# Attention scores with queries on the partitions, and the weights turned by transposing transfers

## The chip, the core and the metric

The kernel runs on one NeuronCore of a Trainium2 chip. A core has TensorE (PE, the matrix engine; PEld is its weight loading), VectorE (DVE), ScalarE (ACT), GpSimd (POOL), SyncE (SP, which here only issues transfers) and 16 DMA engines. Each engine works through its own instruction stream in order; streams meet only at semaphores. The metric is the time of one execution on the device in microseconds. The kernel before takes 780.97 us (median of 3 runs, 780.57 to 782.66).

## The reference

One transformer layer on x of shape (2, 1024, 256): layernorm, causal attention with 16 query heads and 4 key/value heads over low-rank latents, an int8-quantised feed-forward block, and both added to x. The change lies in the attention:

```
q = concat([q_nope, rope(q_rope)])   # 16 heads, 128 + 64 wide
k = concat([k_nope, rope(k_rope)])   # 4 heads, each used by 4 query heads
attn = einsum('bhqd,bhkd->bhqk', q, k) * scale
attn = where(causal, -inf, attn)     # keys after the query are masked
attn = softmax(attn, axis=-1)
out  = einsum('bhqk,bhkd->bhqd', attn, v) @ W_o
```

The kernel works in the latent space: keys are 64 rotated and 64 latent rows, values are 64 latent columns and a column of ones, which gives the sum of the softmax beside the product.

## The kernel before

**Stages.** A prologue makes the latents, joined weights and first queries; a loop of 32 steps (4 key heads x 2 batches x 4 query heads) does the attention; the feed-forward block stands at the end. Small pieces of other work (rounding and turning of integers, rotated keys of later heads, the output product) are spread over the loop through one PSUM bank, `misc`, used in turns by TensorE and one reader (`misc_of`, `misc_used`, `misc_full`).

**A step** handles 1024 queries against 1024 keys, of which the causal half is computed: 8 tiles of 128 keys, 36 blocks of 128 x 128. Precision is bought by splitting: queries, keys and weights are each a high and a low part.

- TensorE first computes, a step or two ahead, the scores with high parts only and queries on the partitions (`max_unit`), into two banks `pmax`. VectorE takes each row's masked maximum (`maxima`, line 863). A transposition of 8 columns (line 1234), a split into two bf16 rows (lines 870, 872) and two transfers (line 368) turn the maxima into a row `m_row` along the queries.
- `scores` then computes the scores with **keys on the partitions**: per strip of up to 512 queries a mask product for the diagonal, a pass that adds minus the maximum (`ones_b` x `m_row`) and three passes, high x high, low x high and high x low. There are 12 strips in a step, in three banks that rotate.
- ScalarE takes the exponential twice (lines 684, 685): rounded to f16 as the high part `p_hi`, and in full in PSUM. VectorE subtracts the two to get `p_lo` (line 996).
- With keys on the partitions the weights already lie as the value product wants them: `values` multiplies each block of `p_hi`, `p_hi`, `p_lo` by 65, 64 and 65 columns of values, into the `head` banks. VectorE divides by the sum (`normalise`).
- GpSimd rotates the queries (lines 469 to 478, 4 instructions) and makes their low part (line 484), two to three steps ahead of their use; `q_hi` has three buffers.

Every fourth step has the output product of two pairs of heads (4 tiles, lines 1278 to 1290); the even steps but the first turn the normalised output (line 1275).

## Time and profile before

| what | value |
|---|---|
| median of the 3 runs | 780.97 us (780.57 to 782.66) |
| the profiled execution's own time | 779.53 us |
| its span | 777.7 us |
| PE busy | 729.5 us, 94% |
| DVE busy | 580.6 us, 75% |
| ACT busy | 496.3 us, 64% |
| POOL busy | 420.4 us, 54% |
| bytes moved by DMA | 33.08 MB |

The span runs from the first to the last instruction; the execution's own time holds 1.8 us around it. Busy is the union of an engine's instructions. A PE instruction is shown from its start to the end of its results, so neighbours overlap; what it costs the engine is the distance to the start of the next. The same holds, by less, on ACT and DVE.

### The profile page before, as it was taken

How to read it: one execution, taken by the hardware profiler on the slowest of the kernel's cores; microseconds unless marked ns; L12 is line 12 of the kernel's file. 1: busy time of each engine (PE TensorE's matmuls, PEld its weight loads, DVE VectorE, ACT ScalarE, POOL GpSimd, SP SyncE). 2: the span in 40 equal slices, each digit the busy share in tenths (PEclk: the TensorE clock that was granted, in tenths of full speed). 3: DMA queues.
4: the chain of work that ended last, by engine and by line, in shares of the span. 5: the costliest groups of instructions: out<-in, count | busy, mean ns of one | idle time of the engine just before them, and what ended most of it. 6: DMA issues, size and time to landing. Idle time of an engine off the chain costs nothing.

```text
span 777.7 us, 18089 instructions
## 1 busy us (share of the span) xinstructions
PE 729.5 (94%) x7010; PEld 582.9 (75%) x7084; DVE 580.6 (75%) x1530; ACT 496.3 (64%) x1015; POOL 420.4 (54%) x210
## 2 busy tenths in 40 slices
PE   7996699899999999999999999999999999999856
PEld 5664468688876678878877888788878888887635
DVE  6748478887777777777777768776777787776796
ACT  3555467577556565767577657765776577657754
POOL 4323546666655554676467646764676467620225
PEclk9786699999999999999999999999999999999989
DMA  9754002001300200010001000100000000000003
GB/s 261 256 201 178 1 1 82 16 15 42 124 1 29 82 28 2 21 43 23 2 1 30 1 15 16 42 15 2 1 29 2 1 2 2 2 1 3 14 0 109
DMA packets 20517, 33.08 MB, mean 43 GB/s; under 512 B 2704, under 2 KB 11472, under 8 KB 20304
## 3 DMA queue, kind: packets, MB, share of 16 engines
q1 hardware_dynamic: 19648, 31.34, 12.8%
q8 instruction: 56, 0.92, 0.5%
q10 hardware_dynamic: 784, 0.59, 0.3%
q14 instruction: 29, 0.24, 0.1%
HBM read 21.30 MB, written 10.49 MB: 41 GB/s over the span
## 4 chain that ended last, share of the span: by engine, by line
PE 78%; DVE 10%; issue 4%; ACT 4%; DMA 2%; POOL 1%; SPq 0%; POOLq 0%; ACTq 0%; DVEq 0%
PE psum L1078 74%; PE psum L1275 2%; DMA acc<-in_L_attn_x 2%; DVE hid L1058 1%; DVE small L1027 1%; ACT psum L685 1%; DVE p_lo L996 1%; POOL res L521 1%; ACT p_hi L684 1%; DVE acc L755 1%; PE psum L1101 1%; ACT hid L711 0%; PE psum L1326 0%; DVE kt_a L960 0%; PE psum L1234 0%
## 5 line engine op out<-in xcount | busy, mean ns | idle before, releaser
L684 ACT ACTIVATE p_hi<-psum 128x512 f16<-128x512 f32 (+3 forms) x384 | 187.7, 489 | 169.8 <-PE psum L1078 164.6
L996 DVE TENSOR_TENSOR p_lo<-psum,p_hi 128x512 f16<-128x512 f32 (+3 forms) x384 | 208.4, 553 | 85.7 <-ACT psum L685 84.5
L863 DVE CUSTOM_DVE_ANT_0 junk<-psum,cmask 128x1024 bf16<-128x1024 f32 (+7 forms) x256 | 187.8, 752 | 58.9 <-issue 57.4
L469 POOL TENSOR_TENSOR q_swap<-q_raw,sin_sb 32x1024 f32<-32x1024 f32 x31 | 73.6, 2374 | 228.9 <-ACT q_raw L613 220.5
L685 ACT ACTIVATE psum<-psum 128x512 f32<-128x512 f32 (+3 forms) x384 | 187.2, 487 | 0.0
L1078 PE MATMUL psum<-q_hi,k_hi 128*128 128x512 f32 (+2 forms) x384 | 187.0, 487 | 0.0
L1078 PEld LDWEIGHTS psum<-kv_tok,p_hi 128*128 128x128 f16 x2304 | 116.9, 97 | 53.4 <-issue 38.6
L1078 PE MATMUL psum<-kv_tok,p_hi 128*128 128x65 f16 (+1 forms) x2304 | 151.9, 196 | 0.4 <-DVE p_lo L996 0.4
L1078 PE MATMUL psum<-kv_tok,p_lo 128*128 128x65 f16 x1152 | 138.1, 192 | 0.0
L1078 PE MATMUL psum<-q_hi,k_lo 128*128 128x512 f32 (+2 forms) x384 | 132.1, 344 | 0.0
L1078 PE MATMUL psum<-q_lo,k_hi 128*128 128x512 f32 (+2 forms) x384 | 131.9, 343 | 0.0
L1078 PE MATMUL psum<-k_hi,q_hi 128*128 128x512 f32 (+3 forms) x384 | 106.0, 358 | 11.7 <-DVE small L863 7.7
L1078 PEld LDWEIGHTS psum<-kv_tok,p_lo 128*128 128x128 f16 x1152 | 109.0, 100 | 0.0
L1078 PE MATMUL psum<-m_row,ones_b 128*128 128x384 bf16 (+2 forms) x313 | 100.8, 322 | 1.4 <-DVE p_lo L996 1.4
L1078 PEld LDWEIGHTS psum<-k_hi,q_hi 128*128 128x128 f32 x384 | 65.5, 192 | 32.2 <-DVE small L863 21.3
L484 POOL TENSOR_TENSOR q_lo<-q_raw,q_hi 128x1024 fp32r<-128x1024 f32 x32 | 76.8, 2401 | 15.9 <-PE psum L1078 10.8
L1078 PEld LDWEIGHTS psum<-q_lo,k_hi 128*128 128x128 f32 x384 | 72.7, 189 | 7.3
L1078 PEld LDWEIGHTS psum<-q_hi,k_lo 128*128 128x128 f32 x384 | 73.8, 192 | 4.3
L472 POOL TENSOR_TENSOR q_swap<-q_raw,sin_sb 32x1024 f32<-32x1024 f32 x31 | 74.0, 2388 | 2.4
L475 POOL TENSOR_TENSOR q_raw<-q_raw,cos_sb 64x1024 f32<-64x1024 f32 x31 | 73.9, 2382 | 2.4
L478 POOL TENSOR_TENSOR q_raw<-q_raw,q_swap 64x1024 f32<-64x1024 f32 x31 | 73.6, 2375 | 2.4
L1078 PEld LDWEIGHTS psum<-q_hi,k_hi 128*128 128x128 f32 x384 | 73.9, 193 | 0.0
(172 smaller groups left out, 1205.8 us busy)
## 6 DMA issues: line engine op xcount, KB each, us to landing
wq_split<-w_split SPq DMA_DIRECT2D x4, 1024.0 KB, 5.5
k_rotated<-k_split SPq DMA_DIRECT2D x8, 512.0 KB, 3.7
wq<-wq_split SPq DMA_DIRECT2D x16, 256.0 KB, 2.7
acc<-in_L_attn_x SPq DMA_DIRECT2D x4, 512.0 KB, 7.7
ffn_t<-in_L_attn_W_o SPq DMA_DIRECT2D x1, 2048.0 KB, 20.7
k_hi<-k_rotated SPq DMA_DIRECT2D x8, 256.0 KB, 4.0
k_lo<-k_rotated SPq DMA_DIRECT2D x8, 256.0 KB, 4.5
w_split<-in_L_ffn_w SPq DMA_DIRECT2D x2, 1024.0 KB, 6.0
```

Of the source, the lines that this page charges most:

```text
L469: pool.tensor_tensor(q_swap[0:HR, :], raw[HR:ROPE, :], sin_sb[HR:ROPE, :], ALU.mult)\
L472: pool.tensor_tensor(q_swap[HR:ROPE, :], raw[0:HR, :], sin_sb[0:HR, :], ALU.mult)\
L475: pool.tensor_tensor(raw[0:ROPE, :], raw[0:ROPE, :], cos_sb[0:ROPE, :], ALU.mult)\
L478: pool.tensor_tensor(raw[0:ROPE, :], raw[0:ROPE, :], q_swap[:, :], ALU.add).then_inc(S["pool_step"], 1)
L484: pool.tensor_tensor(q_lo[s % 2][:, :], q_raw[s % 2][:, :], q_hi[n % QRING][:, :], ALU.subtract)\
L521: pool.tensor_tensor(y[:, :, :], y[:, :, :], acc[:, t:t + 2, :], ALU.add).then_inc(S["f_res"], 1)
L684: act.activation(p_hi[j % PRING][:, o:o + used], src, ACT.Exp, scale=SCALE)
L685: act.activation(src, src, ACT.Exp, scale=SCALE).then_inc(S["exp_done"], 1)
L863: ins = dve.tensor_tensor_reduce(junk[:, o:o + w], pmax[:, o:o + w], cmask[:, T - w:T], 1.0, LOWEST, ALU.add, ALU.max, mcol[:, s % 2, i:i ...
L996: dve.tensor_tensor(p_lo[j % PRING][:, o:o + used], score[c % SBANKS][:, w - used:w], p_hi[j % PRING][:, o:o + used], ALU.subtract).then_i ...
L1078: ins = pe.matmul(dst, lhs, rhs, start=start, stop=stop, skip_group_check=True)
L1275: ins = pe.transpose(misc[:, i * P:(i + 1) * P], o_norm[:, 4 * k + i, :], identf[:, :])
```

## The change

The separate pass for maxima goes, with `pmax`, `m_row`, `m_cast`, their transposition and transfers. The three-pass scores are computed with **queries on the partitions**. VectorE reduces each tile's scores to the negative maximum (line 875 of the new kernel), which ScalarE takes as the bias of the exponential. Now the weights lie the wrong way for the value product and have to be turned:

- the four wide query tiles (7, 6, 5, 4: 1024, 896, 768, 640 keys) keep two exponentials and a subtraction; high and low part stand side by side in one of three buffers `p_src`, and **one transposing DMA per tile** (SP, line 369) turns both into `pt_big`: 512, 448, 384 and 320 KB, 26 blocks of each part per step;
- the four narrow tiles (3 to 0, 10 blocks) take one exponential in f32 into `p_f32`; VectorE makes both halves at once (`small_halves`: a cast, line 891, and a subtraction, line 893, of 1280 columns); TensorE transposes the 20 blocks through `misc` in turns of 8, 8 and 4, and ScalarE copies them to `pt_small` (line 688).

Wide tiles use two regions of PSUM alternately, the narrow ones one bank. The value products of tiles 6, 5, 4 and of the narrow tiles come in the next step; those of tile 7 at the end of the same step. The lookahead of the queries shrinks: queries are projected two steps ahead instead of three, `q_hi` has two buffers, and GpSimd rotates one step ahead. The output product's four tiles are spread over two steps, and a step's leftovers follow the last one. The scale moves from the exponential to the copy of the queries.

```diff
@@ tables
+UNITS = ((7,), (3,), (6,), (2,), (5,), (1, 0), (4,))
+NS = len(UNITS)
+BIG = {7: 0, 6: 1, 5: 2, 4: 3}
+SMALL = {3: 0, 2: 1, 0: 2}
+NB = len(BIG)
+MAX_AT = {i: k for k, i in enumerate(i for unit in UNITS for i in unit)}
+PSRC = 3
+COLS = {7: 0, 5: 0, 6: 2 * CH, 4: 2 * CH + P, 3: 4 * CH, 2: 4 * CH, 1: 4 * CH, 0: 4 * CH + 2 * P}
+KEYS = {7: (CH, CH), 6: (CH, CH - P), 5: (CH, 2 * P), 4: (CH - P, 2 * P), 3: (CH,), 2: (CH - P,), 1: (2 * P,), 0: (2 * P,)}
+OFF = {3: 0, 2: 4 * P, 1: 7 * P, 0: 9 * P}
+WB = 10 * P
+BLOCKS = [(h, i, j) for h in range(2) for i in (3, 2, 1, 0) for j in range(i + 1)]
+TURNS_B = [BLOCKS[k:k + 8] for k in range(0, len(BLOCKS), 8)]
+PV_AT = {0: (6, 1), 2: (5, 1), 3: (4, 1), 6: (7, 0)}
+PV_SMALL = 4
+PV_DONE = {7: 1, 6: 2, 5: 3, 4: 4}
+PV_STEP = 5
...
@@ SyncE
-            def row_of_maxima(n, s):
-                sp.wait_ge(S["m_cast_done"], n + 1)
-                for k in range(2):
-                    sp.dma_start(m_row[s % 2][k:k + 1, :], m_cast[:, k, :]).then_inc(S["m_row_in"], 16)
+            def turn_big(n, i):
+                q, w = NB * n + BIG[i], (i + 1) * P
+                if n:
+                    sp.wait_ge(S["pv_done"], PV_STEP * (n - 1) + PV_DONE[i])
+                sp.wait_ge(S["lo_done"], q + 1)
+                sp.dma_start(pt_big[i][:, :, :], p_src[q % PSRC][:, 0:2 * w], transpose=True)\
+                  .then_inc(p_in[q % PSRC], 16)
...
@@ GpSimd
-            rotate(2, 2, 6)
             for n in range(LAST):
+                if n + 1 < LAST:
+                    rotate(n + 1, n + 1, misc_index(n - 1, "query", 1) + 1 if n else 4)
                 for _, kind, k in misc_of(n):
                     if kind == "kb":
                         keys_low(k)
-                if n + 3 < LAST:
-                    rotate(n + 3, n + 3, misc_index(n, "query", 1) + 1)
-                if n + 2 < LAST:
-                    pool.wait_ge(S["score_done"], NC * (n + 1))
-                    query_low(n + 2, n + 2)
+                if n + 1 < LAST:
+                    query_low(n + 1, n + 1)
...
@@ ScalarE
-                            act.activation(p_hi[j % PRING][:, o:o + used], src, ACT.Exp, scale=SCALE)
-                            act.activation(src, src, ACT.Exp, scale=SCALE).then_inc(S["exp_done"], 1)
+            def exponentials(n, u):
+                for i in UNITS[u]:
+                    w, nb = (i + 1) * P, sm["mcol"][:, NT * (n % 2) + i:NT * (n % 2) + i + 1]
+                    src = psum[:, COLS[i]:COLS[i] + w]
+                    act.wait_ge(S["max_done"], NT * n + MAX_AT[UNITS[u][-1]] + 1)
+                    if i in BIG:
+                        q = NB * n + BIG[i]
+                        if q >= PSRC:
+                            act.wait_ge(p_in[q % PSRC], 16 * (q // PSRC))
+                        act.activation(p_src[q % PSRC][:, 0:w], src, ACT.Exp, bias=nb)
+                        act.activation(src, src, ACT.Exp, bias=nb).then_inc(S["exp_done"], 1)
+                    else:
+                        if n:
+                            act.wait_ge(S["small_lo"], n)
+                        ins = act.activation(p_f32[:, OFF[i]:OFF[i] + w], src, ACT.Exp, bias=nb)
+                        if i in SMALL:
+                            ins.then_inc(S["small_free"], 1)
+            def small_turned(k, idx):
+                act.wait_ge(S["misc_full"], idx + 1)
+                m = len(TURNS_B[k])
+                act.activation(pt_small[:, 8 * k:8 * k + m, :],
+                               misc.bitcast(F16)[:, 0:m * P].rearrange("p (t q) -> p t q", q=P), ACT.Copy)\
+                   .then_inc(S["misc_used"], 1)
...
@@ VectorE
-            def maxima(n, s, u):
-                dve.wait_ge(S["max_done"], USES * n + (u + 1))
-                dve.memset(sm["tick"], 0.0)
-                for i, o in MAX_UNITS[u]:
-                    w = (i + 1) * P
-                    ins = dve.tensor_tensor_reduce(junk[:, o:o + w], pmax[:, o:o + w], cmask[:, T - w:T], 1.0, LOWEST,
-                                                   ALU.add, ALU.max, mcol[:, s % 2, i:i + 1])
-                ins.then_inc(S["max_read"], 1)
+            def maxima(n, u):
+                dve.wait_ge(S["score_done"], NS * n + u + 1)
+                for i in UNITS[u]:
+                    dve.tensor_reduce(sm["mcol"][:, NT * (n % 2) + i:NT * (n % 2) + i + 1],
+                                      psum[:, COLS[i]:COLS[i] + (i + 1) * P], AX.X, ALU.max, negate=True)\
+                       .then_inc(S["max_done"], 1)
+            def big_low(n, i):
+                q, w = NB * n + BIG[i], (i + 1) * P
+                dve.wait_ge(S["exp_done"], q + 1)
+                dve.tensor_tensor(p_src[q % PSRC][:, w:2 * w], psum[:, COLS[i]:COLS[i] + w], p_src[q % PSRC][:, 0:w],
+                                  ALU.subtract).then_inc(S["lo_done"], 1)
+            def small_halves(n):
+                dve.wait_ge(S["small_free"], len(SMALL) * (n + 1))
+                if n:
+                    dve.wait_ge(S["misc_full"], misc_index(n, "pt", 2) + 1)
+                dve.tensor_copy(p_small[:, 0, :], p_f32[:, :]).then_inc(S["small_hi"], 1)
+                dve.wait_ge(S["small_hi"], n + 1)
+                dve.tensor_tensor(p_small[:, 1, :], p_f32[:, :], p_small[:, 0, :], ALU.subtract).then_inc(S["small_lo"], 1)
...
+            for n in range(LAST + 1):
+                s, r = n % STEPS, n % REP
+                for j in range(NS):
+                    if n < LAST:
+                        if j == 4:
+                            big_low(n, 6)
+                            if n:
+                                normalise(n - 1, 1)
                         if j == 6:
-                            turned = misc_index(n, "turn", 1) + 1 if r % 2 == 0 and n > 0 else None
-                            normalise(2 * n + 2, NT * n + PRING + 4, 0, s % 2, turned)
-            end = LAST
-            normalise(2 * end + 1, NT * end + PRING, 1, 1, None)
-            dve.wait_ge(S["pv_done"], NT * end + PRING)
+                            big_low(n, 5)
+                        maxima(n, j)
+                        if j == 2:
+                            big_low(n, 7)
+                    elif j == 4:
+                        normalise(n - 1, 1)
+                    if n and j == 0:
+                        big_low(n - 1, 4)
+                    if n and j == 5:
+                        normalise(n - 1, 0)
...
+                    if n < LAST and j == 6:
+                        small_halves(n)
...
@@ TensorE
-                mm(o, ones_b[:, 0:P], m_row[s % 2][:, qs], not diagonal, False)
-                mm(o, k_hi[b][:, ks], qh[:, qs], False, False)
-                mm(o, k_lo[b][:, ks], qh[:, qs], False, False)
-                mm(o, k_hi[b][:, ks], ql[:, qs], False, True, S["score_done"])
+                    qs, k0 = slice(i * P, (i + 1) * P), 0
+                    for w in KEYS[i]:
+                        ks = slice(k0, k0 + w)
+                        o = psum[:, COLS[i] + k0:COLS[i] + k0 + w]
+                        diagonal = k0 <= i * P < k0 + w
+                        if diagonal:
+                            mm(o[:, i * P - k0:(i + 1) * P - k0], ident[:, :], cmask[:, :], True, False)
+                        mm(o, qh[:, qs], k_hi[b][:, ks], not diagonal, False)
+                        mm(o, qh[:, qs], k_lo[b][:, ks], False, False)
+                        ins = mm(o, ql[:, qs], k_hi[b][:, ks], False, True)
+                        k0 += w
+                ins.then_inc(S["score_done"], 1)
...
+            def turn_small(m, k, idx):
+                pe.wait_ge(S["small_lo"], m + 1)
+                pe.wait_ge(S["misc_used"], idx)
+                for t, (h, i, j) in enumerate(TURNS_B[k]):
+                    o = OFF[i] + j * P
+                    ins = pe.transpose(misc.bitcast(F16)[:, t * P:(t + 1) * P], p_small[:, h, o:o + P], ident16[:, :])
+                ins.then_inc(S["misc_full"], 1)
```

How VectorE's stream reads around the start of a step before (`junk` and `m_cast` belong to the maxima, `ISA` is the masked maximum and its read-out):

```order
L996 TENSOR_TENSOR p_lo0<-psum,p_hi0 128x512 [waits pv_done,exp_done]
L870 TENSOR_SCALAR m_cast<-psum 8x128 [waits m_row_in,max_done]
L872 SCALAR_TENSOR_TENSOR m_cast<-psum,m_cast 8x128 [waits m_split]
L996 TENSOR_TENSOR p_lo1<-psum,p_hi1 128x384 [waits m_cast_done,pv_done,exp_done]
L860 MEMSET small 128x1 [waits max_done]
L863 ISA junk,small<-psum,cmask 128x1024
L863 ISA small 128x1
L996 TENSOR_TENSOR p_lo2<-psum,p_hi2 128x256 [waits pv_done,exp_done]
L888 RECIPROCAL small<-psum 128x4 [waits pv_done]
L892 TENSOR_TENSOR o_norm<-psum,small 128x4x64 [waits norm_step]
```

and in the changed kernel, from the halves of the narrow tiles of one step (`p_small`) into the next:

```order
L891 CAST p_small<-p_f32 128x1280 [waits misc_full,small_free]
L893 TENSOR_TENSOR p_small<-p_f32,p_small 128x1280 [waits small_hi]
L875 TENSOR_REDUCE small<-psum 128x1 [waits score_done]
L883 TENSOR_TENSOR p_src1<-psum,p_src1 128x640 [waits exp_done]
L875 TENSOR_REDUCE small<-psum 128x1 [waits score_done] x2
L883 TENSOR_TENSOR p_src2<-psum,p_src2 128x1024 [waits exp_done]
L916 TENSOR_TENSOR acc<-psum,acc 128x512 [waits acc_in,misc_full]
L875 TENSOR_REDUCE small<-psum 128x1 [waits score_done]
L883 TENSOR_TENSOR p_src0<-psum,p_src0 128x896 [waits exp_done]
L900 RECIPROCAL small<-psum 128x4 [waits pv_done]
L904 TENSOR_TENSOR o_norm<-psum,small 128x4x64 [waits norm_step]
L875 TENSOR_REDUCE small<-psum 128x1 [waits score_done]
```

The low parts stood one behind another with maxima of later steps between them; now each maximum and low part belongs to the step itself, and the halves of the narrow tiles stand between tile 4's maximum and the next tile 7's.

On TensorE, a strip of scores before, with a unit of the maxima pass behind it:

```order
L1078 MATMUL psum<-ident,cmask 128x128 [waits lo_done]
L1078 MATMUL psum<-m_row0,ones_b 128x512
L1078 MATMUL psum<-q_hi0,k_hi1 128x512
L1078 MATMUL psum<-q_hi0,k_lo1 128x512
L1078 MATMUL psum<-q_lo0,k_hi1 128x512
L1078 MATMUL psum<-k_hi1,q_hi1 128x512 [waits max_read]
L1078 MATMUL psum<-k_hi1,q_hi1 128x384
```

and in the changed kernel the end of tile 6's values, behind the scores of tile 7, and what follows (`ident16,p_small` are the transpositions of the narrow tiles):

```order
L1083 MATMUL psum<-kv_tok,pt_big6 128x64
L1083 MATMUL psum<-kv_tok,pt_big6 128x65
L1282 MATMUL psum<-ident16,p_small 128x128 [waits misc_used,small_lo]
L1282 MATMUL psum<-ident16,p_small 128x128 x7
L1083 MATMUL psum<-cmask,ident 128x128 [waits small_free]
L1083 MATMUL psum<-k_hi0,q_hi0 128x512
L1083 MATMUL psum<-k_lo0,q_hi0 128x512
L1083 MATMUL psum<-k_hi0,q_lo0 128x512
L1282 MATMUL psum<-ident16,p_small 128x128 [waits misc_used,small_lo]
L1282 MATMUL psum<-ident16,p_small 128x128 x7
L1083 MATMUL psum<-k_hi0,q_hi0 128x512 [waits lo_done]
```

The pass of `m_row` and the maxima pass are gone; 20 transpositions per step, which wait for `small_lo` and `misc_used`, stand between the scores.

## Rows read from the trace of the kernel before

**Rows 1.** Window: length; busy PE, PEld, DVE, ACT, POOL; PE clock, DMA share, GB/s.
```profile
300.00:400.00 100.00, 100.00 (x1067) 82.59 (x1078) 75.98 (x221) 66.43 (x145) 60.47 (x26) 1.00 0.07 18
```

**Rows 2.** The page's groups: busy us, mean ns, then idle before and its releaser.
```profile
L1078 PE MATMUL psum<-k_hi,q_hi 128*128 128x512 f32 (+3 forms) x384 | 106.0, 358 | 11.7 <-DVE small L863 7.7
L1078 PE MATMUL psum<-m_row,ones_b 128*128 128x384 bf16 (+2 forms) x313 | 100.8, 322 | 1.4 <-DVE p_lo L996 1.4
L863 DVE CUSTOM_DVE_ANT_0 junk<-psum,cmask 128x1024 bf16<-128x1024 f32 (+7 forms) x256 | 187.8, 752 | 58.9 <-issue 57.4
```

**Rows 3.** Timeline of ACT, once a step: start us, length us, what.
```profile
306.47 1.04 ACT L617 ACTIVATE q_hi<-q_raw 128x1024 fp32r<-128x1024 f32 x1
...
324.65 1.05 ACT L617 ACTIVATE q_hi<-q_raw 128x1024 fp32r<-128x1024 f32 x1
...
341.89 1.05 ACT L617 ACTIVATE q_hi<-q_raw 128x1024 fp32r<-128x1024 f32 x1
...
382.85 1.04 ACT L617 ACTIVATE q_hi<-q_raw 128x1024 fp32r<-128x1024 f32 x1
```

**Rows 4.** Timeline of PE: one strip's passes, then blocks of the value product.
```profile
711.77 0.22 PE L1078 MATMUL psum<-ident,cmask 128*128 128x128 bf16 x1
711.83 0.38 PE L1078 MATMUL psum<-m_row,ones_b 128*128 128x512 bf16 x1
...
712.74 0.34 PE L1078 MATMUL psum<-m_row,ones_b 128*128 128x384 bf16 x1
...
715.64 0.22 PE L1078 MATMUL psum<-kv_tok,p_hi 128*128 128x65 f16 x2
...
715.73 0.22 PE L1078 MATMUL psum<-kv_tok,p_hi 128*128 128x65 f16 x2
```

**Rows 5.** Timeline of ACT (beside a row of Rows 3), then of DVE.
```profile
340.89 0.60 ACT L684 ACTIVATE p_hi<-psum 128x512 f16<-128x512 f32 x1 [0.69 <-PE psum L1078]
341.38 0.59 ACT L685 ACTIVATE psum<-psum 128x512 f32<-128x512 f32 x1
...
342.84 0.48 ACT L684 ACTIVATE p_hi<-psum 128x384 f16<-128x384 f32 x1
...
158.06 1.22 DVE L863 CUSTOM_DVE_ANT_0 junk<-psum,cmask 128x1024 bf16<-128x1024 f32 x1
...
159.21 0.08 DVE L863 DVE_READ_ACCUMULATOR2_ANT small<- 128x1 f32 x1
```

**Rows 6.** Timelines of POOL and DVE, and line 960's ns (min/median/max).
```profile
144.94 2.36 POOL L478 TENSOR_TENSOR q_raw<-q_raw,q_swap 64x1024 f32<-64x1024 f32 x1
147.53 2.53 POOL L484 TENSOR_TENSOR q_lo<-q_raw,q_hi 128x1024 fp32r<-128x1024 f32 x1 [0.24 <-POOL q_raw L478]
...
144.99 2.86 DVE L966 TENSOR_SCALAR acc<-acc,small 128x1024 f32<-128x1024 f32 x1
...
157.36 0.74 DVE L966 TENSOR_SCALAR acc<-acc,small 128x1024 f32<-128x1024 f32 x1
...
L960 DVE TENSOR_TENSOR kt_a<-kt_a,kt_b x6: 691/888/969, 104.1 to 276.1; 128x512 f32<-128x512 f32 x6
```

**Rows 7.** Timelines of ACT and PE around the start of the loop.
```profile
78.82 1.91 ACT L643 ACTIVATE ffn_t<-w_split 128x2048 bf16<-128x2048 f32 x1
...
87.45 2.18 ACT L639 ACTIVATE w_split<-w_split,small 128x1024 f32<-128x1024 f32 x2
...
94.50 0.26 PE L1078 MATMUL psum<-ident,cmask 128*128 128x128 bf16 x1
...
95.42 0.63 PE L1078 MATMUL psum<-q_hi,k_lo 128*128 128x512 f32 x1
95.84 0.63 PE L1078 MATMUL psum<-q_lo,k_hi 128*128 128x512 f32 x1
```

**Rows 8.** The page's DMA parts: packets, MB, share; then KB each, us to landing.
```profile
q1 hardware_dynamic: 19648, 31.34, 12.8%
...
k_rotated<-k_split SPq DMA_DIRECT2D x8, 512.0 KB, 3.7
```

More of the change, by code:

```diff
@@ L104 @@
+LARGEST_AT = {(0, 3): 0, (0, 5): 1, (1, 1): 2, (1, 3): 3}
+ROUND_AT = {(2, 1): 0, (2, 3): 1, (2, 4): 2, (2, 5): 3}
+MISC_BASE = 4
 LAST = HKV * STEPS
 def misc_of(n):
-    usual = [x for x in MISC[n % REP] if not (x[1] == "query" and n + 3 >= LAST) and not (x[1] != "query" and n < 2)]
-    return sorted(EXTRA.get(n, []) + usual, key=lambda x: x[0])
-MISC_AT = {(n, kind, k): i for i, (n, kind, k) in enumerate((n, kind, k) for n in range(LAST)
+    r, usual = n % REP, []
+    if n >= 1:
+        usual += [(k, "pt", k) for k in range(3)]
+    if n + 2 < LAST:
+        usual += [(3, "query", 0), (5, "query", 1)]
+    if n < LAST:
+        if r in (0, 2) and n >= 2:
+            usual += [(5, "turn", 1), (6, "turn", 0)]
+        if r == 1 and n > REP:
+            usual += [(4, "out", 0), (6, "out", 1)]
+        if r == 2 and n > REP:
+            usual += [(2, "out", 2), (4, "out", 3)]
+    return sorted(usual + EXTRA.get(n, []), key=lambda x: x[0])
@@ L877, in pmax_use @@
-            def pmax_use(n, s, u):
-                if u < NU:
-                    maxima(n, s, u)
-                else:
-                    cast_maxima(n)
-            def normalise(n2, pv, half, odd, turned):
+            def maxima(n, u):
[4 more added lines that the diff above has]
+                       .then_inc(S["max_done"], 1)
@@ L890, in normalise @@
-                if turned is not None:
-                    dve.wait_ge(S["misc_full"], turned)
+                dve.wait_ge(S["norm_step"], 2 * m + (1 if half else 2))
+                if odd == 0 and m >= 2:
+                    dve.wait_ge(S["misc_full"], misc_index(m, "turn", 0) + 1)
                 dve.tensor_tensor(o_norm[:, 4 * half:4 * half + 4, LAT * odd:LAT * odd + LAT], hb[:, :, 0:LAT],
@@ new lines, in values, with small_values @@
+            def values(m, i):
+                q = NB * m + BIG[i]
+                if i == 7 and m:
+                    pe.wait_ge(S["head_read"], 2 * m - 1)
+                pe.wait_ge(p_in[q % PSRC], 16 * (q // PSRC + 1))
+                tile_values(m, i).then_inc(S["pv_done"], 1)
+            def small_values(m, idx):
+                if m:
+                    pe.wait_ge(S["head_read"], 2 * m)
+                pe.wait_ge(S["misc_used"], idx + 1)
+                for i in (3, 2, 1, 0):
+                    ins = tile_values(m, i)
+                ins.then_inc(S["pv_done"], 1)
```

456 lines of the change are left out of this document (172 added, 284 removed).

## The prediction

> **What bounds the kernel now.** I read the windows first: in the loop TensorE is busy 100% at the full clock, VectorE 76%, ScalarE 66%, GpSimd 60%, the DMA engines 7% [rows 1]. Then the page's groups: the two things that the change removes from TensorE are a maxima pass (busy 106.0 us) and the pass of `m_row` (100.8 us), and from VectorE the masked maximum, 187.8 us [rows 2]. Busy overlaps there, so the price of an instruction is read from the timeline: a strip of 512 with four passes costs 712.74 - 711.83 = 0.91 us, 0.23 a pass, the mask 0.06 and a block of the value product 0.09 [rows 4]. Last the length of a step: `q_hi` is made once a step, and four steps take 382.85 - 306.47 = 76.4 us, of which one without turned outputs or output product, a quiet one, takes 341.89 - 324.65 = 17.2 [rows 3]. The four hold 76.4 - 4 x 17.2 = 7.4 us of the rest. TensorE's own work in a quiet step by these prices: four passes over 4,736 columns 8.5, the maxima pass 2.1, eight masks 0.5, ten passes of queries 2.3, 36 blocks of values 3.3, in all 16.7 of 17.2. TensorE bounds it, and nothing else does.
>
> **What each engine has to do in a quiet step afterwards.** TensorE: three passes 6.4, masks 0.5, queries 2.3, values 3.3, and 20 transpositions of 128 columns at the mask's 0.06, 1.2: 13.7 us. ScalarE costs 0.49 for 512 columns and 0.95 for 1024 [rows 3, 5], so 0.03 and 0.90 per thousand: two exponentials of the wide tiles 6.2, one of the narrow ones 1.3, the copies of 2,560 turned columns 2.4, queries and `q_hi` 1.9: 11.8. VectorE costs 1.15 for 1024 columns from PSUM [rows 5]: maxima over 4,608 columns 5.2, low parts over 3,328 3.7, the cast of 1,280 columns 0.9 (0.74 for 1024 where it runs alone [rows 6]), the subtraction beside it 1.45, normalising about 1: 12.3. GpSimd as before five instructions of 2.4 [rows 6], 12.0. So no engine is full any more. What sets the step is the order in which they wait for each other.
>
> **The chain.** Before, the scores were ready to be used as soon as they came, since the maxima had been made a step ahead. Now every tile goes TensorE, VectorE, ScalarE twice, VectorE, and only then is its PSUM region free; the streams are in fixed order, and the queries' low part, which the first scores of the next step wait for, is made behind `q_hi`, which stands on ScalarE behind tile 5's exponentials. From the moment the halves of the narrow tiles are ready, in us: turning 8 blocks with drain and hand-over 0.8; copy 0.95; exponentials of tile 7 1.9; copy 0.95; third turning 0.55; copy 0.49; exponentials of tile 6 1.68; hand-over 0.15; low part of 6 1.0; normalising 0.5; maximum of 5 0.87; hand-over 0.15; exponentials of 5 1.44; `q_hi` 0.95; hand-over 0.15; GpSimd's low part 2.4; hand-over 0.06. That is 15.0 (hand-overs of 0.06 to 0.1 are my estimate; the drain of 0.2 is 0.63 long against 0.42 to the next start [rows 7]). In front of it stands either the start of the step, scores of 7 and values of 6 (1.43 + 0.63 = 2.1), which makes 17.1, or, when the halves come late, the rest of the step before on VectorE (about 1.2 into the step) and the halves themselves (2.35), 18.6. I take 18.0. Turned outputs and output products lay on TensorE in full before and partly beside other work afterwards, but each makes TensorE, ScalarE and VectorE hand over in `misc` once more, so I leave their 7.4: four steps 79.4, 3.0 more than before, eight times: **+24 us**. The 4.4 us per step that TensorE is spared buy nothing because TensorE then waits.
>
> **GpSimd against VectorE.** VectorE's in-place scaling of 1024 columns took 0.74 us alone and 2.86 when it was started at 144.99, 0.05 after a GpSimd instruction that ended at 147.30: it ended 0.55 behind it. The next GpSimd instruction took 2.53 instead of 2.4. A sum of two SBUF operands (line 960) varies between 0.69 and 0.97 [rows 6]. So VectorE's work that reads SBUF alone waits for a running GpSimd instruction. Before, hardly any stood in the loop. Now the cast and the subtraction do, once a step, on the chain's late entrance, and GpSimd starts its four rotations exactly when it has made the low part, that is when the step begins. The cast waits for the rest of a 2.4 us instruction, 1.2 on average; the subtraction follows a semaphore, so that the next rotation may take its turn first, another 2.4 or nothing. Bounds 0 and 3.6 per step; I take 1.2 and half of 2.4, 2.4 x 32 = **+77 us**. The Trainium skill (SBUF, State Buffer: "SBUF: two separate sides") calls the shared pair of ports an exclusive lock, taken also by a VectorE operation with two SBUF inputs, and the loser "fully blocks". By that rule the sum would take 3.6 a step, 115 us; the trace agrees for the in-place operation (2.86 against 0.74) and shows at most 0.28 more on the sum of two operands.
>
> **The transposing transfers.** 26 blocks of each part are 1.70 MB a step. No row shows such a transfer. Below, the nearest is a plain 512 KB in 3.7 us to landing [rows 8]; tile 7's low part is done some 7 us before its values are wanted, the others' 6 to 9, so the transfer hides with 2 to 3 us to spare; a buffer of `p_src` comes free after three tiles, more than 10 us. Above: each row of 128 f16 might go as a packet of its own at the mean packet's 0.128 x 16 x 777.7 / 19,648 = 0.081 us [rows 8]; 6,656 packets over 16 engines are 33.7 us a step. I take the plain end, 0 us, as the nearest in size, and keep the other for the range; if landing takes 6.5 us instead of 3.7 the cover is gone and each further us costs about one per step. The Trainium skill (DMA: Bandwidth & Descriptors, "Latency and other measured facts") gives 261 GB/s for one measured transposing kernel, an estimate of 2.0 us for tile 7's data, by which the sum would stay; no run here shows it. SP's queue has otherwise few entries, and its waits fall in the tiles' own order; the 64 transfers of `m_row` go.
>
> **Ends of the loop.** The loop starts on TensorE at 94.50. Its prologue no longer holds the first maxima and third queries; it then waits for ScalarE's second set of weights: 80.73, the end of the first, plus 2.18 and 1.91, 84.8: **-9.6** (78.82 + 1.91, and the rows at 87.45 and 94.50) [rows 7]. Behind the last step stand its halves, turning, copies, the last transfer and the values, about 5 us more than before: **+5**. Diagonal masks, key reloads, scale in the copy, smaller buffers: 0, they replace equals or lie on queues with room.
>
> **Sum.** In the profiled execution's own terms 779.5 + 24 + 77 - 9.6 + 5 = 876, which I give as 875. The median of the three runs is 1.4 above that execution, less than I can tell. About 0.3% (2.3 us) is what a measurement tells from no change.
>
> **Rivals.**
> - *Collisions at either bound.* Without them the sum is 799, with all of them 914. Same mechanism, my own range: 795 to 925. With the forecast 0.64.
> - *The transfers bind.* From a landing over 7 us, or a rate under 1.70 MB per 20 us = 85 GB/s, values and `p_src` wait. 0.081 us per row gives 33.7 x 32 = 1,078 for the loop, with 85 before and 55 behind about 1,220; halfway, with landing at 9 us, 876 + 32 x 2.5 = 956. For it: the trace has no such transfer. Against: a plain 512 KB is quick, the engines idle at 7%. 0.18.
> - *TensorE loses its clock.* It would be busy 13.7 of some 20.5 us with pauses of up to 3. After the prologue's waits a pass of 512 costs 0.42, not 0.23 [rows 7], that is 1.2 and not 2.4 GHz. At that clock the 13.7 are about 25 a step: 32 x 25 + 85 + 55, 940. Against: the pauses are short. 0.08.
> - *The other side: TensorE stays the bound.* If the streams' lookahead hides the hand-overs (halves early, collisions beside the path, turned outputs beside it too), the step falls under 19.0 on average, the point from which it is faster. At the early entrance, 17.1 + 1.85, it is 19.0 and with the prologue 770; with all waits hidden 13.7 + 1.85 = 15.5, 32 x 3.6 less, 660. For it: every engine has room. Against: the chain of 15 us has no slack that the streams' order could use. 0.08; 0.02 for no change.
>
> **Numbers.** Predicted 875. The range 800 to 1010 takes nearly all of the forecast, the clock, and the milder half of the transfers. Faster 0.08, same 0.02, slower 0.90.
>
> **What would show it.** Right: TensorE busy well under 90% in the loop, waiting at the small transpositions for the subtraction (line 893) and at scores of 7 for GpSimd's low part; steps of 19 to 23 us; cast and subtraction together between 3 and 6 us with GpSimd busy beside them; the loop beginning near 85; transfers landing in 3 to 6 us. Wrong: waits of the values for DMA, or casts of 0.9 us throughout, or a step under 19.

## The result and the profile after

The changed kernel takes 930.38 us (median of three runs, 927.99 to 933.1) against 780.97 (780.57 to 782.66): ratio 1.191, 95% interval 1.185 to 1.197. The forecast was 875 with a range of 800 to 1010, slower. Direction and mechanism came out, the size fell 55 us short. The profiled execution's span is 931.3 against 777.7, so 153.6 us have to be found.

A stretch of the loop first (length; busy PE, PEld, DVE, ACT, POOL; PE clock, DMA share, GB/s), after:

```profile
300.00:400.00 100.00, 81.50 (x748) 63.00 (x748) 64.61 (x83) 53.27 (x73) 49.63 (x20) 0.81 0.43 77
```

TensorE was busy 100% at full clock [rows 1]; now 81.5%, at a mean clock of 0.81. No other computing engine has gained a share; only the DMA engines have, from 7% to 43%. When every computing engine is idle more than before, a chain of waits sets the time. The page's chain and groups (busy us, mean ns, then idle before and its releaser) say which:

```profile
PE 43%; DVE 30%; ACT 17%; issue 6%; DMA 3%; POOL 1%; POOLq 0%; SPq 0%; ACTq 0%; DVEq 0%
...
L875 DVE TENSOR_REDUCE small<-psum 128x1 f32<-128x1024 f32 (+7 forms) x256 | 189.6, 751 | 116.9 <-PE psum L1083 116.5
...
L1083 PE MATMUL psum<-k_hi,q_hi 128*128 128x512 f32 (+2 forms) x384 | 177.3, 462 | 26.4 <-POOL q_lo L482 13.5
...
L1282 PE MATMUL psum<-ident,p_small 128*128 128x128 f16 x640 | 71.6, 272 | 99.9 <-DVE p_small L893 94.4
...
L893 DVE TENSOR_TENSOR p_small<-p_f,p_small 128x1280 f16<-128x1280 f32 x32 | 108.7, 3398 | 1.1
...
L473 POOL TENSOR_TENSOR q_raw<-q_raw,cos_sb 64x1024 f32<-64x1024 f32 x31 | 92.6, 2987 | 2.4
```

The maxima pass and the `m_row` pass of [rows 2] are gone, as the change says; the maximum costs VectorE 189.6 us against 187.8. TensorE now waits 94.4 us for one instruction, the subtraction on the narrow tiles, and there is one such wait in each of the 32 steps. That subtraction takes 3,398 ns on average.

The length of a step is read as in [rows 3], from `q_hi`, once a step. After, sixteen steps apart:

```profile
449.07 1.06 ACT L613 ACTIVATE q_hi<-q_raw 128x1024 fp32r<-128x1024 f32 x1
...
823.03 1.06 ACT L613 ACTIVATE q_hi<-q_raw 128x1024 fp32r<-128x1024 f32 x1
```

That is 373.96 / 4 = 93.5 us for four steps, against 76.4; eight times the difference is +137 of the 153.6. One collision, in a single step (start us, length us, what; first POOL, then DVE, then PE):

```profile
479.84 2.38 POOL L470 TENSOR_TENSOR q_swap<-q_raw,sin_sb 32x1024 f32<-32x1024 f32 x1
482.29 2.80 POOL L473 TENSOR_TENSOR q_raw<-q_raw,cos_sb 64x1024 f32<-64x1024 f32 x1
485.17 3.49 POOL L476 TENSOR_TENSOR q_raw<-q_raw,q_swap 64x1024 f32<-64x1024 f32 x1
...
480.75 2.15 DVE L891 CAST p_small<-p_f 128x1280 f16<-128x1280 f32 x1
482.93 3.51 DVE L893 TENSOR_TENSOR p_small<-p_f,p_small 128x1280 f16<-128x1280 f32 x1
...
487.50 0.81 DVE L883 TENSOR_TENSOR p_src<-psum,p_src 128x640 f16<-128x640 f32 x1
...
486.50 1.03 PE L1282 MATMUL psum<-ident,p_small 128*128 128x128 f16 x8 [4.46 <-DVE p_small L893]
```

The cast, 0.81 at its shortest, ends 0.68 after the GpSimd instruction that was running (482.22). The subtraction, 1.49 at its shortest, ends 1.35 after the next one (485.09). The GpSimd instruction behind that takes 3.49 instead of 2.4, and ends 2.2 after the subtraction. The two engines take turns, an instruction each, and VectorE gets its turn only behind a whole GpSimd instruction. The last VectorE row shown lies wholly inside that long GpSimd instruction (it ends at 488.66) and loses nothing: 0.81 us, as this subtraction takes everywhere in the loop (807 ns on average, with GpSimd at work beside it in nearly every step). One of its operands is in PSUM. TensorE stands still for 4.46 us. The same stretch by windows:

```profile
482.00:484.00 2.00, 0.05 (x2) 0.00 (x0) 1.97 (x2) 0.00 (x0) 1.92 (x2) 1.00 0.35 65
484.00:486.00 2.00, 0.00 (x0) 0.00 (x0) 2.00 (x1) 0.00 (x0) 1.92 (x2) 0.63 0.00 0
486.00:488.00 2.00, 1.50 (x11) 1.41 (x12) 2.00 (x3) 0.43 (x1) 2.00 (x1) 0.50 0.00 0
488.00:490.00 2.00, 2.00 (x12) 1.48 (x11) 1.00 (x2) 2.00 (x3) 0.66 (x1) 0.50 0.21 43
490.00:492.00 2.00, 2.00 (x11) 1.22 (x11) 0.00 (x0) 2.00 (x3) 0.00 (x0) 0.66 0.64 121
492.00:494.00 2.00, 2.00 (x43) 1.84 (x41) 1.93 (x2) 1.23 (x3) 0.00 (x0) 1.00 0.00 0
```

TensorE stops at 482, its granted clock falls to 0.50 (1.2 GHz) while it waits, and it comes back to work at half speed until about 491. So the pause is paid twice: first as idle time, then as slow products. This is one of the long pauses: over the 32 steps they average 94.4 / 32 = 2.95 us.

The transposing transfers landed not far from the 3.7 us of the plain one that the prediction took for them (line 369: issue ns min/median/max, first and last start; who waited, us and times; landing):

```profile
L369 SPq DMA_TRANSPOSE pt_big<-p_src x128: 1253/1441/5682, 98.6 to 870.0; - x128
...
  PEld psum L1083: 2.7, 4
  PE psum L1083: 2.6, 4
...
DMA to landing us min/median/max: 3.3/4.2/9.1
```

### The profile page after: what moved, and what is told of

It reads as the page before. It is cut to its first block, busy times and chain, and to the rows that moved or that the text cites. A ratio compares the mean times of both kernels' runs of the same rounds, so it can differ in the third digit from the quotient of the medians.

```text
span 931.3 us, 16783 instructions
## 1 busy us (share of the span) xinstructions
PE 731.0 (78%) x6919; PEld 569.7 (61%) x6922; DVE 650.4 (70%) x826; ACT 527.7 (57%) x727; POOL 463.2 (50%) x210
## 4 chain that ended last, share of the span: by engine, by line
PE 43%; DVE 30%; ACT 17%; issue 6%; DMA 3%; POOL 1%; POOLq 0%; SPq 0%; ACTq 0%; DVEq 0%
PE psum L1083 35%; DVE p_small L893 12%; PE psum L1282 6%; DVE p_small L891 5%; ACT p_src L675 4%; ACT pt_small L688 4%; DVE small L875 3%; ACT psum L676 3%; DVE p_src L883 2%; DMA pt_big<-p_src 2%; ACT q_raw L608 1%; DVE o_lo L910 1%; DVE hid L1063 1%; ACT q_hi L613 1%; PE psum L1290 1%
## 5 line engine op out<-in xcount | busy, mean ns | idle before, releaser
L875 DVE TENSOR_REDUCE small<-psum 128x1 f32<-128x1024 f32 (+7 forms) x256 | 189.6, 751 | 116.9 <-PE psum L1083 116.5
L1083 PE MATMUL psum<-k_hi,q_hi 128*128 128x512 f32 (+2 forms) x384 | 177.3, 462 | 26.4 <-POOL q_lo L482 13.5
L675 ACT ACTIVATE p_src<-psum,small 128x1024 f16<-128x1024 f32 (+3 forms) x128 | 121.8, 951 | 52.9 <-DVE small L875 51.1
L1282 PE MATMUL psum<-ident,p_small 128*128 128x128 f16 x640 | 71.6, 272 | 99.9 <-DVE p_small L893 94.4
L1083 PE MATMUL psum<-k_lo,q_hi 128*128 128x512 f32 (+2 forms) x384 | 144.1, 375 | 0.0
L1083 PE MATMUL psum<-k_hi,q_lo 128*128 128x512 f32 (+2 forms) x384 | 144.1, 375 | 0.0
L883 DVE TENSOR_TENSOR p_src<-psum,p_src 128x1024 f16<-128x1024 f32 (+3 forms) x128 | 129.8, 1014 | 15.9 <-ACT psum L676 15.6
L676 ACT ACTIVATE psum<-psum,small 128x1024 f32<-128x1024 f32 (+3 forms) x128 | 118.6, 926 | 0.0
L893 DVE TENSOR_TENSOR p_small<-p_f,p_small 128x1280 f16<-128x1280 f32 x32 | 108.7, 3398 | 1.1
L1083 PE MATMUL psum<-kv_tok,pt_big 128*128 128x65 f16 (+1 forms) x2496 | 103.8, 197 | 3.2 <-DMA pt_big<-p_src 2.6
L1083 PEld LDWEIGHTS psum<-kv_tok,pt_big 128*128 128x128 f16 x2496 | 88.3, 100 | 25.9 <-issue 20.8
L473 POOL TENSOR_TENSOR q_raw<-q_raw,cos_sb 64x1024 f32<-64x1024 f32 x31 | 92.6, 2987 | 2.4
L1083 PEld LDWEIGHTS psum<-k_hi,q_lo 128*128 128x128 f32 x384 | 80.6, 210 | 9.3
```

What stands on the lines that cost most here:

```text
L473: pool.tensor_tensor(raw[0:ROPE, :], raw[0:ROPE, :], cos_sb[0:ROPE, :], ALU.mult)\
L675: act.activation(p_src[q % PSRC][:, 0:w], src, ACT.Exp, bias=nb)
L676: act.activation(src, src, ACT.Exp, bias=nb).then_inc(S["exp_done"], 1)
L875: dve.tensor_reduce(sm["mcol"][:, NT * (n % 2) + i:NT * (n % 2) + i + 1], psum[:, COLS[i]:COLS[i] + (i + 1) * P], AX.X, ALU.max, negate=True)\
L883: dve.tensor_tensor(p_src[q % PSRC][:, w:2 * w], psum[:, COLS[i]:COLS[i] + w], p_src[q % PSRC][:, 0:w], ALU.subtract).then_inc(S["lo_done" ...
L893: dve.tensor_tensor(p_small[:, 1, :], p_f32[:, :], p_small[:, 0, :], ALU.subtract).then_inc(S["small_lo"], 1)
```

## The experiments

Eleven kernels ran, in three groups, each with the kernel before on the same chip (medians 780.1, 781.6 and 780.8). Ratios are to it, with their 95% intervals. The questions were: how much do the collisions cost, how much the clock, what is the transfers' share, and what makes up the rest?

**1. Rotation left out.** The four rotation instructions of `rotate` on GpSimd go:

```
-                pool.tensor_tensor(q_swap[0:HR, :], raw[HR:ROPE, :], sin_sb[HR:ROPE, :], ALU.mult)\
...
                 pool.sem_inc(S["rotated"], 1)
```

> Leaves out GpSimd's four rotations in 31 of 32 steps (the queries stay unrotated); every wait stays. Theory A (collisions of VectorE's cast and subtraction with the rotations, on the path): both fall to their free times, 0.85 and 1.45 us instead of 1.5 and 3.5, which is 2.6 us a step, 84 us of the changed kernel's 930: 846, and less, 800 to 840, if TensorE's shorter pause also keeps its clock. Rival B (the hand-overs themselves set the step, the collisions are beside the path): 915 to 930. Rival C (the transfers set it): 930.

823.69 us, ratio 1.056 (1.051 to 1.060): 107 us gone, as theory A says for the case that TensorE keeps its clock (0.948 over the span, against 0.870).

**2. Rotation later.** The same work, begun when the narrow halves are done:

```
                 if n + 1 < LAST:
+                    if n:
+                        pool.wait_ge(S["small_lo"], n)
                     rotate(n + 1, n + 1, misc_index(n - 1, "query", 1) + 1 if n else 4)
```

> Nothing left out: GpSimd's rotations of a step wait until the halves of the narrow tiles are made. Theory A: cast and subtraction at 0.85 and 1.45, 2.6 us a step saved, but the rotations end some 3 us later and the low part of the queries must still be ready in time: 810 to 860. Rival B: 915 to 930. Rival D (the rotations then come too late for the query chain): above 880 with the cast and subtraction short all the same.

824.97 us, ratio 1.058 (1.056 to 1.060). First the cast of the changed kernel, then the groups of this one, and the mean clock beside its span:

```profile
L891 DVE CAST p_small<-p_f 128x1280 f16<-128x1280 f32 x32 | 48.6, 1517 | 2.2 <-ACT p_f L680 2.2
```

```profile
L1284 PE MATMUL psum<-ident,p_small 128*128 128x128 f16 x640 | 54.0, 225 | 43.7 <-DVE p_small L895 24.6 <-ACT pt_small L690 19.1
...
L895 DVE TENSOR_TENSOR p_small<-p_f,p_small 128x1280 f16<-128x1280 f32 x32 | 47.7, 1492 | 1.1
...
L893 DVE CAST p_small<-p_f 128x1280 f16<-128x1280 f32 x32 | 35.6, 1112 | 1.3 <-ACT p_f L682 1.0
...
core 0: 824.8 us, clock 0.940
```

The subtraction takes 1,492 ns instead of 3,398, the cast 1,112 instead of 1,517: 2.31 us a step, 74 us in 32. (The expected 0.85 for the cast did not come: 24 of the 32 casts took 0.82, but eight, one in four, which met the making of the queries' low part on GpSimd, still took 2.0.) All GpSimd work is still done, and the time is that of experiment 1 within 2 us, so what cost 105 us was when the rotation ran, not that it ran. The other 31 us are not in VectorE's rows; the mean clock went from 0.870 to 0.940.

**3. Plain copies instead of transposing transfers.** (The transposed tiles are thus not transposed; a reciprocal is replaced by an addition of the same cost, so that no value overflows.)

```
-sp.dma_start(pt_big[i][:, :, :], p_src[q % PSRC][:, 0:2 * w], transpose=True)
+sp.dma_start(pt_big[i][:, :, :], p_src[q % PSRC][:, 0:2 * w].rearrange("p (t q) -> p t q", q=P))
```

> The transposing transfers become plain copies of the same bytes, and the reciprocal an addition of the same size: weights stay unturned and sums undivided, the output is not the reference's. Theory A (transfers are hidden): 925 to 932 us, landing near 3.7 us instead of 4.2, nothing moves. Rival C (the transfers or their packets set the step): well under 900.

927.77 us, ratio 1.189 (1.186 to 1.192), which is within the noise of the changed kernel's 1.191, although the plain copies of tile 7 landed in 2.9 us (those of the other tiles in 2.5 to 2.9; the transposing ones in 4.2) and cost 0.46 us to issue against 1.44:

```profile
L369 SPq DMA_DIRECT2D pt_big<-p_src x128: 464/465/547, 94.0 to 865.3; - x128
...
pt_big<-p_src SPq DMA_DIRECT2D x32, 512.0 KB, 2.9
```

**4. Products that nothing reads, in TensorE's pause.** 32 products of 128 columns into a free bank ahead of the wait for `small_lo`, the collisions left as they are:

```
+                if k == 0:
+                    pe.wait_ge(S["small_free"], len(SMALL) * (m + 1))
+                    for _ in range(32):
+                        mm(bank[4][:, 0:P], ones_b[:, 0:P], ones_b[:, 0:P], True, True)
                 pe.wait_ge(S["small_lo"], m + 1)
```

> Nothing left out; TensorE does 32 extra products of 128 columns into the narrow tiles' bank ahead of its wait for the halves, where it idles 3 us a step. Theory A with the clock as a second cost (granted clock 0.87 over the span, 0.5 for some us behind the pause): the clock stays up, 0.95 or more, and 20 to 45 us come back: 885 to 910. Rival E (the clock costs nothing because TensorE waits anyway): 928 to 935, and up to 960 if the extra products are themselves in the way.

900.12 us, ratio 1.157 (1.150 to 1.164): more work, 30 us less.

```profile
L893 DVE TENSOR_TENSOR p_small<-p_f,p_small 128x1280 f16<-128x1280 f32 x32 | 109.0, 3406 | 1.1
...
core 0: 897.2 us, clock 0.950
```

The subtraction is as slow as before (3,406), the clock is 0.950. So the clock's share is about 30 us by itself (26, give or take 7, by the two ratios with their intervals). That is also what experiment 2 leaves beyond VectorE's rows: 105 - 74 = 31.

**5. Narrow tiles read from PSUM.** ScalarE makes the upper half and the full value as for the wide tiles, VectorE subtracts from PSUM, the cast goes:

```
-                        ins = act.activation(p_f32[:, OFF[i]:OFF[i] + w], src, ACT.Exp, bias=nb)
+                        act.activation(p_small[n % 2][:, 0, OFF[i]:OFF[i] + w], src, ACT.Exp, bias=nb)
+                        act.activation(src, src, ACT.Exp, bias=nb).then_inc(S["small_exp"], 1)
...
+                ins = dve.tensor_tensor(ps[:, 1, OFF[i]:OFF[i] + w], psum[:, COLS[i]:COLS[i] + w],
+                                        ps[:, 0, OFF[i]:OFF[i] + w], ALU.subtract)
```

> The four narrow tiles are handled as the four wide ones are: ScalarE writes the upper half and the full value, VectorE subtracts with the full value in PSUM and one operand in SBUF; the cast of 1,280 columns is gone. Theory (only VectorE instructions with all operands in SBUF lose time to GpSimd's rotation): no VectorE instruction on the narrow tiles is above about 1.3 us, its total falls by some 75 us against the changed kernel, and the time is as with the rotation moved, 810 to 835; the extra exponentials (some 1.3 us a step on ScalarE) may cost up to 20 of it. Rival (the loss comes with GpSimd being busy, whatever VectorE reads): 915 to 930, and the subtractions are lengthened as before.

886.59 us, ratio 1.132 (1.127 to 1.138). Half of the theory held, and the time did not:

```profile
L472 POOL TENSOR_TENSOR q_raw<-q_raw,cos_sb 64x1024 f32<-64x1024 f32 x31 | 73.3, 2363 | 2.4
...
L1089 PE MATMUL psum<-cmask,ident 128*128 128x128 bf16 x256 | 59.7, 233 | 80.3 <-DVE p_small L891 80.2
...
L891 DVE TENSOR_TENSOR p_small<-psum,p_small 128x512 f16<-128x512 f32 x32 | 21.8, 681 | 0.0
```

The largest subtraction takes 681 ns, and the rotation's third instruction 2,363 instead of 2,987, with the rotation at its old place: with one operand in PSUM neither engine lengthens the other. (Few of these largest subtractions met GpSimd at work; those of tiles 1 and 0, which nearly all did, lost nothing either.) But the four narrow tiles share a PSUM bank, which now stays taken until VectorE has subtracted, and TensorE waits 80.2 us for it with the scores of the next tile. I had priced the extra exponentials and not the bank.

**6. Two transfers for a tile instead of one.**

```
-                sp.dma_start(pt_big[i][:, :, :], p_src[q % PSRC][:, 0:2 * w], transpose=True)\
+                for h in range(2):
+                    sp.dma_start(pt_big[i][:, h * (i + 1):(h + 1) * (i + 1), :], p_src[q % PSRC][:, h * w:(h + 1) * w],
+                                 transpose=True).then_inc(p_in[q % PSRC], 16)
```

> Each wide tile is turned by two transfers, one for each half, instead of one. Theory (the transfers lie beside other work): within 1% of the changed kernel, 925 to 938; the queue's issues double, 4 us a step more on SyncE, which has nothing else to do. Rival (the turning transfer is on the chain, as 3% of it suggest): each half lands sooner or later by 1 us and the time moves by 15 us or more, either way.

931.34 us, ratio 1.190 (1.183 to 1.197). No change: that both halves go in one transfer neither costs nor brings anything here.

**7. Both edits of 2 and 4.**

> Both earlier edits in one: the rotation starts behind the narrow halves, and TensorE computes 32 products of 128 columns that nothing reads ahead of its wait for them. Theory (what is left over the kernel before is the chain of waits, with a small share of the clock): granted clock 0.96 to 0.99 against 0.94, products at full clock, 800 to 818. Rival (the 45 us left are the chain alone and the clock follows it): 823 to 830, or more since the products take 1.7 us a step of TensorE.

853.81 us, ratio 1.090 (1.084 to 1.096), 29 us slower than experiment 2, though the clock rose from 0.940 to 0.956. That is the rival's "or more". With the rotation moved, TensorE waits for the halves in only 23 steps, 24.6 us in all (the row of experiment 2), 1.1 us each; the products take 1.7, more than such a pause, and lengthen the step. In these two runs the products paid where the pauses were 2.95 us on average, and cost where they were 1.1.

**8. Shorter rotation instructions.** The same rotation, same place, 256 columns at a time:

```
+                    for c in range(0, T, T // 4):
+                        cc = slice(c, c + T // 4)
+                        ins = pool.tensor_tensor(out[:, cc], x[:, cc], y[:, cc], op)
+                    ins.then_inc(S["pool_step"], 1)
```

> The same rotation at the same place, in 16 instructions of 256 columns instead of four of 1,024; nothing is left out. Theory A (the VectorE instruction waits for the end of the GpSimd instruction that is under way, once): the subtraction is 1.49 us plus at most one of 0.6 us, 1.9 to 2.2 us in place of 3.40, the cast 1.1 to 1.5, and the time 860 to 890. Theory B (the two share the path to memory in proportion while both are at work): the subtraction stays at 2.8 to 3.5 us and the time at 915 to 935.

847.76 us, ratio 1.083 (1.077 to 1.088), 83 us faster than the changed kernel:

```profile
L474 POOL TENSOR_TENSOR q_raw<-q_raw,cos_sb 64x256 f32<-64x256 f32 x124 | 86.9, 728 | 2.4
...
L892 DVE TENSOR_TENSOR p_small<-p_f,p_small 128x1280 f16<-128x1280 f32 x32 | 60.0, 1876 | 1.1
...
L890 DVE CAST p_small<-p_f 128x1280 f16<-128x1280 f32 x32 | 41.8, 1305 | 1.3 <-ACT p_f L679 1.0
```

The subtraction loses 0.38 us to GpSimd (1,876 - 1,492) instead of 1.9, although GpSimd is busier than ever (62% of the span). The loss goes with the length of one GpSimd instruction, not with GpSimd's load: a wait for a turn. This is theory A; B is out. The time itself came out 12 us under theory A's range; the clock rose too, from 0.870 to 0.931.

**9. Moved rotation, `q_hi` a unit earlier** (`QHI_SLOT` 3 instead of 4).

> The rotation behind the narrow halves (825 us), and ScalarE's rounding of the next query one unit earlier in the step. Theory (what is left over the kernel before is the chain through the narrow tiles, to which the query's lower half does not belong): 820 to 830. Rival (with the rotation moved back GpSimd's lower half comes late, and TensorE's 9 waits of up to 1.8 us for it set the step): 805 to 818.

815.63 us, ratio 1.042 (1.036 to 1.048), 9 us better than experiment 2 and the best version found that leaves nothing out; inside the rival's range and outside the theory's. It is still 4% slower than the kernel before. TensorE's 9 waits for the queries' low part, 12.7 us in experiment 2, are gone, as the rival says. But a second thing went with them. The cast in experiment 2 and here (ns min/median/max):

```profile
L893 DVE CAST p_small<-p_f x32: 815/818/2045, 105.4 to 760.8; 128x1280 f16<-128x1280 f32 x32
...
L893 DVE CAST p_small<-p_f x32: 815/817/827, 103.6 to 744.8; 128x1280 f16<-128x1280 f32 x32
```

With the low part made earlier, no cast meets it any more: eight casts lose 1.2 us less, 9 us in all. Which of the two gave back the 9 us is not separated by this run.

**10. Moved rotation, cast and subtraction left out** after the first step.

> The rotation behind the narrow halves, and VectorE's cast and subtraction on the narrow tiles left out after the first step (their values are stale from then on). Theory (both stand on the chain that sets the step, ahead of TensorE's turning of the narrow blocks): up to 2.6 us a step go, 745 to 800. Rival (after the move TensorE's waits for them are only 24.6 us in 23 steps, and the three turns with ScalarE's copies between them bind): 800 to 822.

797.36 us, ratio 1.021 (1.015 to 1.028). Taking 2.6 us of VectorE off every step gives back 28 us, 0.9 a step. That is inside the theory's range, but only 2.6 us from its upper end, where the rival's begins, and far from its 2.6 us a step: a third of the two instructions' length comes back, and the run does not decide more. Even without them the kernel is 17 us slower than before; that this is the longer way through the other hand-overs is argued, not tested.

**11. Moved rotation, the halves in two parts.**

```
+                c = slice(0, 7 * P) if part == 0 else slice(7 * P, WB)
...
-                    if n < LAST and j == 6:
-                        small_halves(n)
+                    if n < LAST and j in (5, 6):
+                        small_halves(n, j - 5)
```

> The rotation behind the narrow halves, and cast and subtraction in two parts: the first 896 columns a unit earlier, 384 at the old place; nothing is left out. Theory (their 2.6 us stand on the chain): some 1.6 us a step come off it, less 0.2 for the two further instructions, 780 to 805. Rival (the first part only delays VectorE's maximum of the last units by what it takes off behind them): 820 to 835.

845.98 us, ratio 1.081 (1.075 to 1.087): 21 us slower than experiment 2. Its rows of waits (total us, times, longest):

```profile
ACT p_src L677 <- DVE small L877: 104.2, 60, 3.6
...
PE psum L1088 <- DVE p_src L885: 32.9, 21, 2.9
```

ScalarE's wait for the maxima grows to 104.2 from 48.1 us in experiment 2: the early part stands ahead of a maximum on VectorE's queue. The rival held, and more strongly than it said: the time lies 11 us above its range.

## Why the prediction was right, and where it fell short

Of the signs that it named, all came but two by a little: the steps take 23.4 us and not 19 to 23, and the loop begins at 88.6 and not near 85. The terms one by one:

**The chain** (+24). Right in kind, too small. Experiment 2 shows the steps almost without collisions; its `q_hi`, sixteen steps apart:

```profile
397.11 1.06 ACT L615 ACTIVATE q_hi<-q_raw 128x1024 fp32r<-128x1024 f32 x1
...
719.43 1.06 ACT L615 ACTIVATE q_hi<-q_raw 128x1024 fp32r<-128x1024 f32 x1
```

322.32 / 4 = 80.6 us for four steps against the forecast 79.4 and 76.4 before: +34 in 32 steps instead of +24. The window of four of its steps (columns as above):

```profile
397.11:478.26 81.15, 69.43 (x795) 55.43 (x794) 57.52 (x81) 55.19 (x78) 47.45 (x20) 1.00 0.56 94
```

TensorE is busy 69.43 of 81.15 us, at full clock, and so bounds nothing. Where the other 10 us lie, a quiet step of experiment 2 shows:

```profile
521.09 1.06 ACT L615 ACTIVATE q_hi<-q_raw 128x1024 fp32r<-128x1024 f32 x1
...
538.61 1.06 ACT L615 ACTIVATE q_hi<-q_raw 128x1024 fp32r<-128x1024 f32 x1
```

It takes 17.5 us, less than the 18.0 of the forecast, so the whole surplus is in the steps with turned outputs and output products: 80.6 - 4 x 17.5 = 10.6 us instead of the 7.4 that I had left them. That each of them adds hand-overs in `misc` I had seen and priced at nothing; that it is these hand-overs is argued, not tested. (The "4.4 us per step that TensorE is spared" are 4.2 by the prediction's own prices, and 3.0 with the 20 transpositions; the number enters no sum.)

**Collisions** (+77). The mechanism held. Against their shortest, 0.81 and 1.49, the two instructions lost 0.7 and 1.9 us a step, 83 us in all; 74 of these went in experiment 2, the other 9 are its eight long casts and are counted in its +34. Within the total the halves were wrong: I gave the cast 1.2 and the subtraction 1.2. "Another 2.4 or nothing" is, in nearly every step, another 2.4: the median subtraction is 3,516 ns. The full bound, 3.6 a step, was not reached. The Trainium skill (SBUF, State Buffer: "SBUF: two separate sides") says that the loser of the shared ports is fully blocked, also for an operation with two operands in SBUF. The runs agree: no loss with an operand in PSUM (0.81 us inside a GpSimd instruction above, and experiment 5), and in experiment 8 a loss that shrinks with the length of the blocking instruction. The 0.28 us of [rows 6] on a sum of two operands met only the last 0.41 us of a GpSimd instruction (it ended at 276.49), and should have carried no weight against the rule:

```profile
274.11 2.38 POOL L478 TENSOR_TENSOR q_raw<-q_raw,q_swap 64x1024 f32<-64x1024 f32 x1
...
276.08 0.96 DVE L960 TENSOR_TENSOR kt_a<-kt_a,kt_b 128x512 f32<-128x512 f32 x1
```

**TensorE's clock** (a rival at 0.08, nothing in the sum). This is the step that failed. I wrote "against: the pauses are short" and took the clock as all or nothing: the loop at 1.2 GHz throughout, 940 us. It was neither. A collision makes TensorE pause for 1.8 to 4.5 us, and late in nearly each of these pauses, or behind it, the granted clock falls to 0.50, in most steps for 3 to 7 us and in some for 10 to 14. In experiment 4, filling the pause gives back 30 us, and the 31 us of experiment 2 beyond the rows agree. The clock's term belonged in the sum, as a consequence of the collisions: where the halves make TensorE wait 1.1 us on average (24.6 / 23, experiment 2) the clock is 1.00 over the four steps above (0.95 from 93 to 397, where the extra work lies), where they make it wait 2.95 it was 0.81 from 300 to 400. With it the sum would have been 906.

**Transfers** (0). Right. They landed in 4.2 us at the median (9.1 at the longest), inside the cover of some 7; the values waited 2.6 us in all. Experiments 3 and 6 show that the time stays whether they transpose or copy, and in one or in two. The rival at 0.18, and the upper price of 33.7 us a step, are out. The Trainium skill (DMA: Bandwidth & Descriptors, "Latency and other measured facts") has a rate of 261 GB/s, from which I had estimated 2.0 us for the largest; the shortest landing of any was 3.3.

**Prologue** (-9.6) and **end** (+5). TensorE's first scores:

```profile
88.63 0.80 PE L1083 MATMUL psum<-k_hi,q_hi 128*128 128x512 f32 x1 [8.05 <-ACTq L657]
```

88.63 against 94.50 [rows 7]: -5.9. But outside the steady steps the sum says +17 (153.6 - 137), where I had -4.6. Most of it lies in the first steps, which carry extra work (the `EXTRA` table). With `q_hi` of the third step and of the fifteenth, before and then after:

```profile
113.44 1.05 ACT L617 ACTIVATE q_hi<-q_raw 128x1024 fp32r<-128x1024 f32 x1
...
360.12 1.04 ACT L617 ACTIVATE q_hi<-q_raw 128x1024 fp32r<-128x1024 f32 x1
```

```profile
132.81 1.07 ACT L613 ACTIVATE q_hi<-q_raw 128x1024 fp32r<-128x1024 f32 x1
...
449.07 1.06 ACT L613 ACTIVATE q_hi<-q_raw 128x1024 fp32r<-128x1024 f32 x1
```

Twelve steps take 246.68 before, 17.5 more than twelve of 19.1; after they take 316.26, 36 more than twelve of 23.4. So the extra work, key reloads among it, costs 18 us more than it did. I had it at 0, "equals, or on queues with room": the work is equal, but before it lay behind a TensorE that was busy anyway, and now each piece is one more link of the chain. One such piece of the changed kernel, a product for the keys that waits 1.11 us for ScalarE's copy:

```profile
409.33 0.73 PE L1083 MATMUL psum<-k_hi,wkr_hi 64*128 64x512 f32 x1 [1.11 <-ACT pt_small L688]
```

In experiment 2 the same twelve steps take 29.5 us more than twelve of its own 20.1 (from 125.88 to 397.11), so some 12 of the 18 stay without the collisions. No run leaves the extra work out. The rest of the 17 cancels between the start and the end.

**The sum again**, in measured terms: chain 34, collisions 74, clock 30, extra work 18, start and end about 0, together 156 against 153.6. The terms are not independent measurements: chain and extra work are differences of step lengths, and the clock's 30 is at the same time what the steady steps leave over.

## What to carry to other kernels

When an edit takes work off the bounding engine and puts a round trip in its place, add up the round trip, and then ask of every pause that it makes how long it is: here TensorE paid its pauses (3 us a step on average) a second time in part, as slow products (about 1 us a step, 30 in 32). Before a VectorE instruction whose operands all lie in SBUF (a cast, or a sum of two) is put on such a path, look at what GpSimd does at that moment; move the GpSimd work, or cut it into short instructions, and most of the loss goes. "Costs nothing, since the engine has room" holds for an instruction that nobody waits for, not for one on a chain.

## What the runs showed of the hardware

- VectorE and GpSimd took turns by whole instructions: a subtraction of 1,280 columns took 1.49 us alone, 3.40 on average beside GpSimd instructions of 2.4 us, and 1.88 beside instructions of 0.6 to 0.9 us. GpSimd's were lengthened as well (2.99 against 2.37). With one VectorE operand in PSUM there was no loss on either side (0.81 us for 640 columns inside a GpSimd instruction).
- Cutting GpSimd's work into quarters had a price of its own: the instructions on 32 partitions took 0.94 us instead of 2.37 / 4 = 0.59, but the kernel gained 83 us.
- The granted clock fell to 0.50 in a pause of 4.46 us and was 1.00 again 5 us after its end; it fell behind some pauses of 1.8 us too, and not behind others (it did behind the one that ended at 599.4, and not behind the one that ended at 507.2).
- The transposing transfers of 320 to 512 KB took SyncE 1.44 us each to issue (plain ones 0.46) and landed in 4.2 us (plain ones in 2.5 to 2.9).
